# First layer's cross attention moved from the stacked, per-head loop to keys and values folded into its weights

## The chip, the cores and the metric

One core of one Trainium2 chip runs the whole program in a single launch. The metric is device time in microseconds, lower is better. The program is a two-layer decoder, and the change touches one of its six attention or expert stages, and a little of the stage behind it.

## The reference, cut to what matters

There are 4 batches of 512 tokens of width 128, and a context of 4 batches of 77 tokens of width 128. Each of the two layers does self attention, cross attention on the context and a mixture of experts, each added to its input and normalised. What the change touches is the first layer's cross attention and the norms behind it:

```python
def _L0_xattn_ref(q, k, v, Wq, bq, Wk, bk, Wv, bv, Wo, bo):   # HEADS = 16, DK = 8; k = v = the context
    qp = (q @ Wq + bq).reshape(b, s, HEADS, DK).transpose(0, 2, 1, 3)
    kp = k @ Wk + bk                       # (b, 77, 8): one key and one value head, shared by all 16
    vp = v @ Wv + bv
    scores = jnp.einsum('bhqd,bkd->bhqk', qp, kp)
    attn = jax.nn.softmax(scores, axis=-1)
    out = jnp.einsum('bhqk,bkd->bhqd', attn, vp)
    return out.transpose(0, 2, 1, 3).reshape(b, s, d) @ Wo + bo
...
x = _layernorm(x + _L0_xattn_ref(x, ctx_1024, ctx_1024, ...), axis=-1)
# _L0_ffn_ref begins with attention(layer_norm(x, ln1_w, ln1_b), ...): a second norm, with weights
```

The second layer's cross attention has 16 heads of width 64 with their own keys and values, on the same context.

## The kernel before, in words

The stages run one after the other. Each is one or two blocks; a block is one program for each of the five engines, and ends when all engines have ended theirs. Six tags name the stages in the tiles: a, b, c for the first layer's self attention, cross attention and the attention inside its feed-forward part; f for its experts; d, e, g for the second layer's self attention, cross attention and experts. XT holds the activations with width on the partitions, X those with tokens on the partitions.

**Stage b before** is `narrow_cross_attention`, three blocks.
- `narrow_projections` computes the queries for 4 batches (a float32 matmul of 512 columns each), ScalarE adds the bias (L310), VectorE splits each float32 result into three bfloat16 parts (`split_parts`, L185 to L190: cast, subtract, cast, subtract, cast), SyncE stores the parts to device memory (L261) and loads them back as stacks with 8 rows of head width times 9 combinations of parts (`load_stacks`, L353). Beside it `cross_operands` makes keys and values, and GpSimd sets rows 96 to 127 of the key stack KX to 1.0 (L1139); stage c needs these ones, b does not.
- `narrow_cross` runs a hardware loop over 16 steps of 4 heads, 64 heads of 512 tokens in all: scores (L1204), maximum and subtraction (L1266, L1268), exponential (L1292), transposes by TensorE (L1250), copy out of PSUM (L1303), value products (L1237), then the end of a group, with transposes (L385) and a division (L394, L397).
- `finish` projects with Wo, adds X and the bias, does two norms for each batch, and transposes back into XT. `norm_scales` puts the reciprocal root on GpSimd (L858, L860).

**Stage c** starts with `narrow_projections` as well, for queries, keys and values. It has nothing beside it on GpSimd before.

**Stage e** is the form that b takes over: `wide_operands` (L1670 and on) folds keys into the query weights (A, 128 x 77 for each head and batch) and values into the output weights (U); CP holds what the query bias adds, in three bfloat16 parts. `flat_cross` then has 32 halves: a tile of 128 tokens by 8 heads. Its order is written out by hand. For each half h TensorE does `turn(h)`, five transposes (L1887), `score(h + 3)`, two float32 matmuls of 308 columns (L1877) each with a small bfloat16 one (L1879), and `weigh(h)`, five matmuls (L1897). VectorE does `lessen(h + 2)` (L1967, L1971), `total(h + 1)` (L1978, L1982) and each second half an addition to X (L1988). ScalarE does the copy out of PSUM (L1938) and the exponential (L1932), GpSimd the division (`normalise`, L1854). Behind each batch of 8 halves the norm of the batch before is put in between: `layer(b, 0)`, statistics (L1992, L1995), at half 2 of the next batch, `layer(b, 1)`, application (L2001), at half 3, and GpSimd does `rstd` (L1848, L1850) behind `normalise` of half 3. For the last batch all of it stands at the end. With `pre` set there are two norms: then `layer(b, 1)` applies the first and takes the statistics of the second, `layer(b, 2)` applies the second, at half 4, and GpSimd does both `rstd` behind `normalise` of half 3, in order. No stage used this path before.

Of the kernel before, what the change touches and what calls it, by code (L numbers as in the profile page):

```python
# [356 lines left out]
def gather_values(c, pool, t, first, s_pv, s_vg, cross_values=None, per_group=1):  # L357


    nc = c.nc  # L360
# [2 lines left out]
    if cross_values is None:
        for kt in range(QT):
            src = c.VN[:, bass.ds((t // GROUPS) * QT + kt, 1), bass.ds((t % GROUPS) * GH * HD8, GH * HD8)]
            last = nc.gpsimd.tensor_copy(c.VG[:, kt, :, 0:HD8], src.rearrange("p a (h d) -> p (a h) d", d=HD8))
    else:
        last = nc.gpsimd.tensor_copy(c.VG[0:SROWS, 0, 0:1, 0:HD8], cross_values[:, bass.ds(t // GROUPS, 1), :])
# [736 lines left out]


def cross_operands(c, tag, own, wk, bk, wv, bv, KX, VB):

    nc = c.nc
    GR = SROWS // HD8  # L1110
    WK = c.sb(f"{tag}_WK", [P, HD8], F32, own)
    WKR = c.sb(f"{tag}_WKR", [P, SROWS], F32, own)
    BK = c.sb(f"{tag}_BK", [SROWS, 1], F32, own)
    WV = c.sb(f"{tag}_oWV", [P, HD8], F32, own)
    BV = c.sb(f"{tag}_oBV", [KC, HD8], F32, own)
    G = c.sb(f"{tag}_G", [SROWS, GR], F32, own)
    MK = c.sb(f"{tag}_MK", [SROWS, NPART], F32, own)
    FULL = c.sb(f"{tag}_KF", [SROWS, B * KC], F32, own)
    PARTS = c.sb(f"{tag}_KP", [SROWS, NPART, B * KC], BF16, own)
    s_w, s_g, s_ops, s_k, s_v, s_split = (c.sem(f"{tag}_o{n}") for n in ("w", "g", "ops", "k", "v", "split"))  # L1120

    def load(sp):
        sp.dma_start(WK[:, :], wk).then_inc(s_w, 16)
        sp.dma_start(WV[:, :], wv).then_inc(s_w, 16)
        sp.dma_start(BV[:, :], row(bv, KC)).then_inc(s_w, 16)
        for g in range(NPART * NPART):
            sp.dma_start(BK[g * HD8:(g + 1) * HD8, :], col(bk)).then_inc(s_w, 16)

    def pool_part(pool):
        nc.gpsimd.memset(VB[:, :, :], 0.0)  # L1130
        nc.gpsimd.memset(G[:, :], 1.0).then_inc(s_g, 1)
        pool.wait_ge(s_g, 1)
        nc.gpsimd.affine_select(out=G[:, :], in_=G[:, :], compare_op=ALU.is_ge, fill=0.0, base=0,
                                pattern=[[-HD8, GR]], channel_multiplier=1).then_inc(s_g, 1)
        pool.wait_ge(s_g, 2)
        nc.gpsimd.affine_select(out=G[:, :], in_=G[:, :], compare_op=ALU.is_ge, fill=0.0, base=HD8 - 1,
                                pattern=[[HD8, GR]], channel_multiplier=-1).then_inc(s_g, 1)
        pool.wait_ge(s_g, 3)
        nc.gpsimd.memset(c.KX[SROWS:P, :, :], 1.0)  # L1139

    def tensor_part(pe):
        pe.wait_ge(s_w, 16 * 12)
        pe.wait_ge(s_ops, 2)
        nc.tensor.matmul(c.ps_s[0:SROWS, 2, 0:B * KC], WKR[:, :], c.CTT[:, :], start=True, stop=True).then_inc(s_k, 1)
        for b in range(B):
            last = nc.tensor.matmul(c.ps_t[0:KC, 0, b * HD8:(b + 1) * HD8], c.CTT[:, b * KC:(b + 1) * KC], WV[:, :],
                                    start=True, stop=True)
        last.then_inc(s_v, 1)

    def vector_part(dve):  # L1150
        ops, split = Chain(s_ops), Chain(s_split)
        dve.wait_ge(s_w, 16 * 12)
        ops.inc(nc.vector.memset(WKR[:, NPART * NPART * HD8:], 0.0))
        ops.inc(nc.vector.tensor_copy(
            WKR[:, 0:NPART * NPART * HD8].rearrange("p (g d) -> p g d", d=HD8),
            WK[:, :].rearrange("p (a d) -> p a d", a=1).broadcast_to([P, NPART * NPART, HD8])))
        dve.wait_ge(s_g, 3)
        g = G[:, 0:NPART * NPART].rearrange("p (i j) -> p j i", j=NPART)
        ops.inc(nc.vector.reduce_sum(MK[:, :], g, AX.X))
        dve.wait_ge(s_k, 1)  # L1160
        rows = NPART * NPART * HD8
        ops.inc(nc.vector.tensor_copy(FULL[:, :], c.ps_s[0:SROWS, 2, 0:B * KC]))
        ops.wait(dve)
        ops.inc(nc.vector.tensor_scalar(FULL[0:rows, :], FULL[0:rows, :], BK[0:rows, :], None, ALU.add))
        ops.wait(dve)
# [1208 lines left out]
```

## Time and profile before

| | us |
|---|---|
| median of 3 runs | 2275.23 (2266.92 to 2277.47) |
| profiled execution, its own time | 2271.61 |
| span of its trace | 2269.9 |
| mean granted TensorE clock | 0.897 of 2.4 GHz |
| stage b: projections, loop, finish | 376.87 to 558.22: 44.39, 101.20, 35.76 |
| projections of stage c | 558.22 to 628.0 |
| stage e: operands, flat loop | 1872.08 to 2053.36: 43.84, 137.44 |

Over the span TensorE is busy for 1775.7 us (78%), its weight loads for 1000.7, VectorE for 1384.8 (61%), ScalarE for 1032.5 (45%), GpSimd for 155.7 (7%). As stages follow one another, these shares say little of one stage. The windows by stage and the instructions in order of time are the views to read.

### The profile page before, as it was taken

How to read it: one execution, taken by the hardware profiler on the slowest of the kernel's cores; microseconds unless marked ns; L12 is line 12 of the kernel's file. 1: busy time of each engine (PE TensorE's matmuls, PEld its weight loads, DVE VectorE, ACT ScalarE, POOL GpSimd, SP SyncE). 2: the span in 40 equal slices, each digit the busy share in tenths (PEclk: the TensorE clock that was granted, in tenths of full speed). 3: DMA queues.
4: the chain of work that ended last, by engine and by line, in shares of the span. 5: the costliest groups of instructions: out<-in, count | busy, mean ns of one | idle time of the engine just before them, and what ended most of it. 6: DMA issues, size and time to landing. Idle time of an engine off the chain costs nothing. (4 is left out here: it accounts for less than half of the span.)

```text
span 2269.9 us, 33575 instructions
## 1 busy us (share of the span) xinstructions
PE 1775.7 (78%) x9665; PEld 1000.7 (44%) x9718; DVE 1384.8 (61%) x4754; ACT 1032.5 (45%) x1970; POOL 155.7 (7%) x281
## 2 busy tenths in 40 slices
PE   4177775584149668699994999999999977997997
PEld 2144443353013223367772444444444434665664
DVE  7388885565358557433335777777777763774445
ACT  3288881362016446433331555656665543332221
POOL 2000003001000000100002000000000001330000
PEclk7599996696659889889996999999999987998999
DMA  1543200510540330010001000000000001000000
GB/s 57 80 44 38 29 0 11 79 25 7 89 51 5 39 41 2 3 38 19 19 10 37 1 1 1 1 1 1 1 0 1 1 1 39 1 1 21 17 19 26
DMA packets 57636, 48.74 MB, mean 21 GB/s; under 512 B 12691, under 2 KB 53047, under 8 KB 57527
## 3 DMA queue, kind: packets, MB, share of 16 engines
q1 hardware_dynamic: 57527, 47.45, 13.0%
q8 instruction: 49, 0.80, 0.1%
q14 instruction: 60, 0.49, 0.1%
HBM read 38.30 MB, written 8.91 MB: 21 GB/s over the span
## 5 line engine op out<-in xcount | busy, mean ns | idle before, releaser
L1432 PE MATMUL ps_s<-d_KZ,d_Q 128*128 128x512 f32 x512 | 265.4, 601 | 16.1 <-issue 6.8
L1580 ACT ACTIVATE d_PR<-d_PR,d_NM 128x512 f32<-128x512 f32 x256 | 184.7, 721 | 189.9 <-DVE d_NM L1511 189.5
L557 DVE TENSOR_REDUCE c_NM<-ps_t 128x1 f32<-128x512 f32 x256 | 169.9, 688 | 96.7 <-PE ps_t L437 95.0
L1507 DVE CUSTOM_DVE_ANT_0 d_PR<-ps_s,d_BH 128x512 f32<-128x512 f32 x256 | 176.2, 688 | 61.5 <-PE ps_t L1440 44.7
L437 PE MATMUL ps_t<-KX,QX 96*128 (+1 forms) x256 | 107.6, 425 | 105.1 <-DVE c_IB L575 47.6
L2288 DVE SCALAR_TENSOR_TENSOR X<-ps_t,GATE,X 128x128 f32<-128x128 f32 x272 | 76.7, 344 | 185.1 <-PE ps_t L2213 185.1
L619 ACT ACTIVATE c_PT<-ps_s 128x1024 f32<-128x1024 f32 x128 | 130.4, 1024 | 126.2 <-PE ps_s L460 124.3
L1440 PEld LDWEIGHTS ps_t<-ident,d_PR 128*128 128x128 f32 x1024 | 121.3, 141 | 150.8 <-issue 132.6
L1587 ACT ACTIVATE d_PT<-ps_t 128x512 f32<-128x512 f32 x256 | 149.9, 586 | 50.6 <-PE ps_t L1440 49.0
L762 ACT ACTIVATE a_PR<-a_PR,a_NM 128x128 f32<-128x128 f32 (+3 forms) x256 | 129.8, 555 | 78.0 <-DVE a_NM L743 78.0
L1440 PE MATMUL ps_t<-ident,d_PR 128*128 128x128 f32 x1024 | 156.4, 275 | 10.1 <-ACT d_PT L1587 8.1
L672 PE MATMUL ps_t<-ident,a_PR 128*128 128x128 f32 x640 | 115.4, 289 | 50.5 <-ACT a_PT L686 38.1
L2250 ACT ACTIVATE f_HT<-ps_s,f_BE 128x512 f32<-128x512 f32 x128 | 87.8, 687 | 128.5 <-PE ps_s L2203 127.7
L2203 PE MATMUL ps_s<-XT,g_W 128*128 128x512 f32 x288 | 131.9, 601 | 1.7 <-DVE g_HT L2267 1.7
L1519 DVE TENSOR_SCALAR d_PR<-d_PR,d_RDEN 128x512 f32<-128x512 f32 x256 | 124.7, 487 | 9.0
L2213 PEld LDWEIGHTS ps_t<-f_W,f_HT 128*128 128x128 f32 x1024 | 119.2, 192 | 14.8 <-issue 14.6
L1452 PE MATMUL ps_v<-d_PT,d_VB 128*64 128x512 f32 x512 | 116.9, 598 | 5.6 <-ACT d_PT L1587 4.9
L2213 PE MATMUL ps_t<-f_W,f_HT 128*128 128x128 f32 x1024 | 119.3, 275 | 0.0
L2203 PE MATMUL ps_s<-XT,f_W 128*128 128x512 f32 x256 | 117.4, 603 | 0.6 <-DMA f_W<-in_L_ffn_w 0.6
L672 PEld LDWEIGHTS ps_t<-ident,a_PR 128*128 128x128 f32 x640 | 70.3, 142 | 96.2 <-ACT a_PT L686 48.0
L2248 ACT ACTIVATE g_GT<-ps_s 128x512 f32<-128x512 f32 x72 | 43.0, 597 | 141.9 <-PE ps_s L2203 141.8
L437 PEld LDWEIGHTS ps_t<-KX,QX 96*128 (+1 forms) x256 | 25.0, 98 | 183.6 <-issue 103.0
(330 smaller groups left out, 3118.2 us busy)
## 6 DMA issues: line engine op xcount, KB each, us to landing
QX<-split_parts SPq DMA_DIRECT2D x108, 128.0 KB
KX<-split_parts SPq DMA_DIRECT2D x72, 128.0 KB
f_W<-in_L_ffn_w SPq DMA_DIRECT2D x16, 256.0 KB, 3.1
split_parts<-a_PARTS SPq DMA_DIRECT2D x8, 384.0 KB, 10.3
split_parts<-c_PARTS SPq DMA_DIRECT2D x8, 384.0 KB, 11.0
g_W<-in_L_ffn_w SPq DMA_DIRECT2D x24, 128.0 KB, 2.2
split_parts<-b_PARTS SPq DMA_DIRECT2D x4, 384.0 KB, 10.7
X<-in_x SPq DMA_DIRECT2D x4, 256.0 KB
```

The source lines that it names most:

```text
L437: nc.tensor.matmul(c.ps_t[:, i % 2, :], QX[0:SROWS, bass.ds(head, 1), qt * P:(qt + 1) * P], KX[0:SROWS, bass.ds(head, 1), :], start=True, ...
L557: nc.vector.tensor_reduce(NM[:, qt, j:j + 1], c.ps_t[:, i % 2, :], AX.X, ALU.max, negate=True).then_inc(maxed, 1)
L619: nc.scalar.activation(PT[:, half, j, :, :], c.ps_s[:, 2 * (j % 2):2 * (j % 2) + 2, :], ACT.Exp).then_inc(exped, 1)
L672: last = nc.tensor.transpose(c.ps_t[:, qt % 2, kt * P:(kt + 1) * P], PR[:, j % 2, qt, kt * P:(kt + 1) * P], c.ident[:, :])
L762: nc.scalar.activation(PR[:, j % 2, qt, 0:k], PR[:, j % 2, qt, 0:k], ACT.Exp, bias=NM[:, j % 2, qt:qt + 1]).then_inc(exped, 1)
L1432: nc.tensor.matmul(c.ps_s[:, qt % 2, :], Q[:, p % 2, qt * P:(qt + 1) * P], KZ[:, p % 2, i % 2, :], start=True, stop=True).then_inc(scores, 1)
L1440: mm = nc.tensor.transpose(c.ps_t[:, qt % 2, kt * P:(kt + 1) * P], PR[:, i % 2, qt, kt * P:(kt + 1) * P], c.ident[:, :])
L1507: nc.vector.tensor_tensor_reduce(out=PR[:, h % 2, qt, :], in0=c.ps_s[:, qt % 2, :], in1=BH[:, h, S - P - qt * P:2 * S - P - qt * P], scale ...
L1580: nc.scalar.activation(PR[:, h % 2, qt, :], PR[:, h % 2, qt, :], ACT.Exp, bias=NM[:, h % 2, qt:qt + 1], accum_out=DEN[:, h % 2, qt:qt + 1] ...
L1587: nc.scalar.activation(PT[:, i // 2 % 2, i % 2, :, qt * P:(qt + 1) * P], c.ps_t[:, qt % 2, :].rearrange("p (k q) -> p k q", q=P), ACT.Copy ...
L2203: nc.tensor.matmul(c.ps_s[:, ch, :], W[:, (ch % CH) * P:(ch % CH + 1) * P], c.XT[:, b * S:(b + 1) * S], start=True, stop=True).then_inc(s_ ...
L2213: mm = nc.tensor.matmul(c.ps_t[:, b % 2, q * P:(q + 1) * P], HT[:, b % 2, ch, q * P:(q + 1) * P], W2[i][:, ch, :], start=(ch == 0), stop=( ...
```

## The change

Stage b becomes two blocks: `narrow_operands`, which is new, and `flat_cross` with `pre` set, so with its two norms in the loop. The projections, the stacks, the loop by heads and the finish of b go. The setting of KX rows 96 to 127 moves to GpSimd in the projections of stage c, where it is the block's first GpSimd instruction.

```diff
@@ narrow_self_attention (stage c calls it without rel, so causal is None)
-            tables = distance_tables(c, rel, *causal, brief) if causal else None
+            tables = distance_tables(c, rel, *causal, brief) if causal else Beside(
+                lambda sp: None, lambda pool: nc.gpsimd.memset(KX[SROWS:P, :, :], 1.0), lambda pe: None, lambda dve: None)
             narrow_projections(c, tag, brief, scratch, QX, KX, s_qx, wq, wk, wv, bq, bk, bv, qscale, beside=tables)
@@ cross_operands, narrow_cross, narrow_cross_attention: removed, as is the cross part of gather_values
@@ new
+def narrow_operands(c, tag, wq, bq, wk, bk, wv, bv, wo, A, CP, U):
...
+            def _(sp):
+                sp.dma_start(WKV[:, 0, :], wk).then_inc(s_w, 16)
+                sp.dma_start(WKV[:, 1, :], wv).then_inc(s_w, 16)
+                sp.dma_start(BKV[:, 0, :], row(bk, 1)).then_inc(s_w, 16)
+                sp.dma_start(BKV[:, 1, :], row(bv, 1)).then_inc(s_w, 16)
+                sp.dma_start(WQ[:, :], wq).then_inc(s_w, 16)
+                sp.dma_start(BQ[:, :], col(bq)).then_inc(s_w, 16)
+                sp.dma_start(WO[:, :], wo).then_inc(s_w, 16)
+                sp.wait_ge(s_split, SPLIT_OPS + 1)
+                for i in range(NPART):
+                    sp.dma_start(CP[i:i + 1, :, :, :].rearrange("a h b k -> a h (b k)"), CH[:, i, :]).then_inc(s_cp, 16)
+                sp.wait_ge(s_cp, 16 * NPART)
...
+            def _(pool):
+                nc.gpsimd.memset(ONE[:, :], 1.0).then_inc(s_one, 1)
+                nc.gpsimd.memset(MH[:, :], 1.0).then_inc(s_mask, 1)
...
+                pool.wait_ge(s_kvout, 1)
+                for b in range(B):
+                    if b >= 2:
+                        pool.wait_ge(s_a, b - 1)
+                    nc.gpsimd.tensor_tensor(KBD[:, b % 2, :, :], over_heads(KV[:, 0, b * KC:(b + 1) * KC], H),
+                                            masks(slice(0, H)), ALU.mult).then_inc(s_kbd, 1)
...
+            def _(pe):
+                pe.wait_ge(s_w, 16 * 7)
+                nc.tensor.transpose(c.ps_f[:, 0:P], WQ[:, :], c.ident[:, :]).then_inc(s_wqt, 1)
+                pe.wait_ge(s_rep, 4)
+                pe.wait_ge(s_one, 1)
+                for w in range(2):
+                    nc.tensor.matmul(c.ps_s[:, w, 0:K2], WREP[:, w, :, :].rearrange("p h d -> p (h d)"), c.CTT[:, :],
+                                     start=True, stop=False)
+                    nc.tensor.matmul(c.ps_s[:, w, 0:K2], BREP[:, w, :, :].rearrange("p h d -> p (h d)"), ONE[:, :],
+                                     start=False, stop=True).then_inc(s_kv, 1)
+                pe.wait_ge(s_kvout, 1)
+                pe.wait_ge(s_bqm, 1)
+                nc.tensor.matmul(c.ps_v[0:H, 0:K2], BQM[:, :], KV[:, 0, :], start=True, stop=True).then_inc(s_c, 1)
...
+                for b in range(B):
+                    pe.wait_ge(s_kbd, b + 1)
+                    if b:
+                        pe.wait_ge(s_aout, b)
+                    for q in range(4):
+                        mm = nc.tensor.matmul(c.ps_s[:, q, 0:4 * KC], WQT[:, :],
+                                              KBD[:, b % 2, 4 * q:4 * q + 4, :].rearrange("p h k -> p (h k)"),
+                                              start=True, stop=True)
+                    mm.then_inc(s_a, 1)
+                    pe.wait_ge(s_vbd, 2 * (b + 1))
+                    if b:
+                        pe.wait_ge(s_uout, 2 * b)
+                    for i in range(2 * CHUNKS):
...
+                        mm = nc.tensor.matmul(dst, VBD[:, b % 2, i // CHUNKS, (i % CHUNKS) * P:(i % CHUNKS + 1) * P],
+                                              WO[:, :], start=True, stop=True)
+                    mm.then_inc(s_u, 1)
...
+            def _(act):
+                act.wait_ge(s_kv, 1)
+                nc.scalar.activation(KV[:, 0, :], c.ps_s[:, 0, 0:K2], ACT.Copy).then_inc(s_kvout, 1)
...
+                for b in range(B):
+                    act.wait_ge(s_a, b + 1)
+                    nc.scalar.activation(A[:, b, :, :].rearrange("p (q m) k -> p q (m k)", q=4), c.ps_s[:, :, 0:4 * KC],
+                                         ACT.Copy).then_inc(s_aout, 1)
...
+            def _(dve):
+                split = Chain(s_split)
+                dve.wait_ge(s_w, 16 * 7)
+                for w in range(2):
+                    nc.vector.tensor_copy(WREP[:, w, :, :], WKV[:, w:w + 1, :].broadcast_to([P, H, HD8])).then_inc(s_rep, 1)
+                    nc.vector.tensor_copy(BREP[:, w, :, :], BKV[:, w:w + 1, :].broadcast_to([1, H, HD8])).then_inc(s_rep, 1)
...
+                def values(b):
+                    if b >= 2:
+                        dve.wait_ge(s_u, b - 1)
+                    for half in range(2):
+                        nc.vector.tensor_tensor(
+                            VBD[:, b % 2, half, 0:HH * KC].rearrange("p (h k) -> p h k", k=KC),
+                            over_heads(KV[:, 1, b * KC:(b + 1) * KC], HH), masks(slice(half * HH, (half + 1) * HH)),
+                            ALU.mult).then_inc(s_vbd, 1)
+
+                def products(b):
+                    dve.wait_ge(s_u, b + 1)
+                    nc.vector.tensor_copy(U[:, b, 0:8, :].rearrange("p (a i) d -> p a (i d)", a=2), c.ps_t[:, :, :]).then_inc(s_uout, 1)
...
+                products(3)
+                split.wait(dve)
+                split_parts(nc, dve, split, CF[:, :], lambda i: CH[:, i, :])
@@ decoder
-            narrow_cross_attention(c, "b", a["L0_xattn_Wq"], a["L0_xattn_bq"], a["L0_xattn_Wk"], a["L0_xattn_bk"],
-                                   a["L0_xattn_Wv"], a["L0_xattn_bv"], scratch)
-            finish(c, "b", "ctx", wo=a["L0_xattn_Wo"], bias=a["L0_xattn_bo"], pre=(a["L0_ffn_ln1_w"], a["L0_ffn_ln1_b"]))
+            with ExitStack() as own:
+                A, CP, U = flat_operand_tiles(c, "b", own)
+                narrow_operands(c, "b", *(a[f"L0_xattn_{n}"] for n in ("Wq", "bq", "Wk", "bk", "Wv", "bv", "Wo")), A, CP, U)
+                flat_cross(c, "b", A, CP, U, a["L0_xattn_bo"], pre=(a["L0_ffn_ln1_w"], a["L0_ffn_ln1_b"]))
```

`flat_cross` itself is not changed.

## Rows read from the trace of the kernel before

**Rows 1.** Windows: us, then busy us (x instructions) of each engine, clock, DMA share, GB/s.
```profile
376.87:421.26 44.39, 8.72 (x18) 4.10 (x18) 24.39 (x35) 2.75 (x4) 14.30 (x5) 0.54 0.35 64
421.26:522.46 101.20, 83.97 (x704) 55.10 (x704) 65.33 (x160) 67.26 (x144) 6.49 (x17) 0.91 0.28 36
522.46:558.22 35.76, 12.85 (x64) 9.79 (x64) 23.43 (x104) 5.50 (x8) 10.13 (x16) 0.63 0.02 4
1872.08:1915.92 43.84, 30.16 (x160) 19.62 (x160) 13.79 (x32) 16.29 (x34) 0.40 (x2) 0.83 0.19 49
1915.92:2053.36 137.44, 126.18 (x688) 83.71 (x688) 93.58 (x192) 44.83 (x68) 49.20 (x46) 0.93 0.01 1
1917.30:1933.80 16.50, 15.93 (x43) 8.35 (x43) 9.11 (x14) 2.74 (x4) 8.00 (x7) 0.51 0.01 4
1938.00:1967.00 29.00, 29.00 (x171) 19.60 (x170) 21.13 (x37) 10.97 (x17) 9.72 (x8) 1.00 0.00 1
```

**Rows 2.** Instructions in order of time, stage b's projections and the start of c's.
```profile
377.81 13.75 POOL L1139 MEMSET KX<- 32x16384 bf16 x1
382.32 9.52 DVE L185 CAST b_PARTS<-b_FULL 128x512 bf16<-128x512 f32 x1 [2.76 <-ACT b_FULL L310]
...
558.22 1.28 SPq L251 DMA_DIRECT2D c_W<-in_L_ffn_w_qkv  x3
563.43 0.50 PEld L283 LDWEIGHTS ps_s<-XT,c_W 128*128 128x128 f32 x2 [6.69 <-DMA c_BV<-in_L_ffn_b_qkv]
566.33 0.43 DVE L185 CAST c_PARTS<-c_FULL 128x512 bf16<-128x512 f32 x1 [2.76 <-ACT c_FULL L310]
```

**Rows 3.** Instructions in order of time, stage e's operands.
```profile
1882.29 1.40 PE L1694 MATMUL ps_s<-CTT,e_Wk 128*128 128x308 f32 x2 [11.10 <-DMA e_Bv<-in_L_xattn_bv]
1883.48 1.23 PE L1698 MATMUL ps_s<-CTT,e_Wv 128*128 128x308 f32 x2
1887.69 0.52 ACT L1745 ACTIVATE e_KT<-ps_s,e_Bk 128x308 f32<-128x308 f32 x1 [1.18 <-PE ps_s L1694]
1898.93 0.31 DVE L185 CAST e_CH<-e_CF 16x308 bf16<-16x308 f32 x1
1900.96 1.84 SPq L1680 DMA_DIRECT2D e_CP<-e_CH  x3
```

**Rows 4.** DMA issues: count, KB each, median us from issue to landing.
```profile
e_CP<-e_CH SPq DMA_DIRECT2D x3, 9.6 KB, 1.9
```

**Rows 5.** Instructions in order of time, stage e's loop where the first norm is put in.
```profile
1969.21 0.58 PEld L1887 LDWEIGHTS ps_t<-ident,e_PR 128*128 128x128 f32 x5
1970.94 1.97 DVE L2001 TENSOR_SCALAR X<-X,e_MV,e_RS 128x128 f32<-128x128 f32 x4
1971.10 1.22 POOL L1854 TENSOR_TENSOR e_PR<-e_PR,e_RDEN 128x616 f32<-128x616 f32 x1 [1.10 <-DVE e_RDEN L1982]
1971.66 1.19 PEld L1897 LDWEIGHTS ps_f<-e_U,e_PT 128*128 128x128 f32 x10
1972.77 0.58 PEld L1887 LDWEIGHTS ps_t<-ident,e_PR 128*128 128x128 f32 x5
1976.74 0.53 PEld L1887 LDWEIGHTS ps_t<-ident,e_PR 128*128 128x128 f32 x5 [0.32 <-POOL e_PR L1854]
```

**Rows 6.** Instructions in order of time, stage b's finish: two norms in a row.
```profile
536.11 1.08 DVE L867 TENSOR_SCALAR X<-b_fR,b_fMV,b_fRS 128x128 f32<-128x128 f32 x4
538.91 1.04 POOL L860 TENSOR_TENSOR b_fRS<-b_fRS,neghalf 128x4 f32<-128x4 f32 x1
546.46 1.04 POOL L860 TENSOR_TENSOR b_fRS<-b_fRS,neghalf 128x4 f32<-128x4 f32 x1
546.67 0.69 DVE L1012 TENSOR_TENSOR b_fR<-b_fR,b_fBO 128x512 f32<-128x512 f32 x1
```

**Rows 7.** Instructions in order of time, the end of stage e.
```profile
2047.43 0.87 DVE L1992 BATCH_NORM_STATS2 e_ST<-X 128x6 f32<-128x128 f32 x4
2050.20 1.11 DVE L2001 TENSOR_SCALAR X<-X,e_MV,e_RS 128x128 f32<-128x128 f32 x4 [1.47 <-POOL e_RS L1850]
```

More of the change, by code:

```diff
@@ L354, in load_stacks, with gather_values @@
                                  scratch[b, w, :, part, :].rearrange("(h d) t -> d h t", d=HD8)).then_inc(sem, 16)
-def gather_values(c, pool, t, first, s_pv, s_vg, cross_values=None, per_group=1):
+def gather_values(c, pool, t, first, s_pv, s_vg, per_group=1):
     nc = c.nc
@@ L362, in gather_values @@
         pool.wait_ge(s_pv, per_group * t)
[L363 to L368, printed above, removed]
+    for kt in range(QT):
+        src = c.VN[:, bass.ds((t // GROUPS) * QT + kt, 1), bass.ds((t % GROUPS) * GH * HD8, GH * HD8)]
+        last = nc.gpsimd.tensor_copy(c.VG[:, kt, :, 0:HD8], src.rearrange("p a (h d) -> p (a h) d", d=HD8))
     last.then_inc(s_vg, 1)
@@ L1089, in narrow_self_attention @@
     with ExitStack() as own:
+        nc = c.nc
         QX, KX = c.QX, c.KX
@@ L1104, in narrow_self_attention @@
             narrow_full_attention(c, tag, own, QX, KX, scratch, s_qx)
[L1107 to L1165, printed above, removed]
-        split_parts(nc, dve, split, FULL[:, :], lambda i: PARTS[:, i, :])
-        kx = KX[:, :, :].rearrange("p b k -> p (b k)")
-        ops.inc(nc.vector.tensor_scalar(kx, PARTS[:, 0, :], MK[:, 0:1], None, ALU.mult))
-        for i in (1, 2):
-            ops.wait(dve)
-            ops.inc(nc.vector.scalar_tensor_tensor(kx, PARTS[:, i, :], MK[:, i:i + 1], kx, ALU.mult, ALU.add))
-        dve.wait_ge(s_v, 1)
-        nc.vector.tensor_tensor(VB[0:KC, :, :], c.ps_t[0:KC, 0, 0:B * HD8].rearrange("p (b d) -> p b d", b=B),
-                                BV[:, :].rearrange("p (a d) -> p a d", a=1).broadcast_to([KC, B, HD8]), ALU.add)
-    return Beside(load, pool_part, tensor_part, vector_part)
@@ L1312, in narrow_cross_attention @@
-def narrow_cross_attention(c, tag, wq, bq, wk, bk, wv, bv, scratch):
-    with ExitStack() as own:
-        QX = c.QX
-        KX = c.sb(f"{tag}_KX", [SROWS, B, KC], BF16, own)
-        VB = c.sb(f"{tag}_VB", [SROWS, B, HD8], F32, own)
-        s_qx = c.sem(f"{tag}_qx")
-        with ExitStack() as brief:
-            operands = cross_operands(c, tag, brief, wk, bk, wv, bv, KX, VB)
-            narrow_projections(c, tag, brief, scratch, QX, None, s_qx, wq, None, None, bq=bq, beside=operands)
-        narrow_cross(c, tag, own, QX, KX, VB, scratch, s_qx)
@@ L2315, in decoder @@
             finish(c, "a", "ctx", wo=a["L0_attn_Wo"], bias=a["L0_attn_bo"])
-            narrow_cross_attention(c, "b", a["L0_xattn_Wq"], a["L0_xattn_bq"], a["L0_xattn_Wk"], a["L0_xattn_bk"],
-                                   a["L0_xattn_Wv"], a["L0_xattn_bv"], scratch)
-            finish(c, "b", "ctx", wo=a["L0_xattn_Wo"], bias=a["L0_xattn_bo"], pre=(a["L0_ffn_ln1_w"], a["L0_ffn_ln1_b"]))
+            with ExitStack() as own:
+                A, CP, U = flat_operand_tiles(c, "b", own)
+                narrow_operands(c, "b", *(a[f"L0_xattn_{n}"] for n in ("Wq", "bq", "Wk", "bk", "Wv", "bv", "Wo")), A, CP, U)
+                flat_cross(c, "b", A, CP, U, a["L0_xattn_bo"], pre=(a["L0_ffn_ln1_w"], a["L0_ffn_ln1_b"]))
             q, k, v = (slice(i * P, (i + 1) * P) for i in range(3))
```

185 lines of the change are left out of this document (67 added, 118 removed).

## The prediction

> **What bounds the kernel now.** I read the windows first, cut at the first instruction of each stage. The stages don't overlap, so a stage's length counts in full. Stage b takes 44.39 + 101.20 + 35.76 = 181.35 us [rows 1]. None of its three blocks is bound by one engine alone all through: the projections have VectorE busy 24.39 of 44.39 us and wait for DMAs; the loop has TensorE busy 83.97 of 101.20 at a granted clock of 0.91; the finish is a chain, with TensorE at 12.85 and VectorE at 23.43 of 35.76. All of this the change removes.
>
> The same windows hold what takes its place, since stage e runs the same loop with the same 32 halves and the same sizes: 43.84 us of operands and 137.44 us of flat loop [rows 1]. There TensorE is busy 126.18 of 137.44 us, and 29.00 of 29.00 us in an undisturbed stretch at full clock. So the flat loop goes at TensorE's pace, a half every 1972.77 - 1969.21 = 3.56 us [rows 5].
>
> Then I read the instructions in order of time. In b's projections one cast of VectorE takes 9.52 us, where c's same cast takes 0.43 us. It ends at 391.84, just behind GpSimd's setting of KX, which runs from 377.81 to 391.56 [rows 2]. VectorE's cast stood still while GpSimd wrote.
>
> **The change part by part.**
>
> *Removed:* 181.35 us, with its stacks, its group ends and that stalled cast.
>
> *Operands of b.* Times from the block's start.
> - Loads: c's six DMAs let TensorE start 563.43 - 558.22 = 5.2 us behind the first issue [rows 2]. Here are seven; one more issue makes 5.4. Bounds 4 and 6.
> - Four small VectorE copies of up to 128 columns stand before the first product. The trace has no such copy; nearest is the 308-column cast at 0.31 [rows 3], so 4 x 0.25 = 1.0; between 0.5 and 1.3.
> - Keys: two accumulating products of 308 columns. At the low clock one follows another after 1883.48 - 1882.29 = 1.19 us [rows 3]: 2.4 us, and 0.6 with ScalarE's 0.52 copy [rows 3]. Keys are there at 9.4.
> - GpSimd spreads the first batch's keys over the heads: 1232 elements in each partition; `normalise` takes 1.22 us for 616 [rows 5], so 2.4. TensorE can begin at 11.8. The value products, at most another 2.4 us, and their copy lie beside this.
> - For each batch TensorE makes A, 4 products of 308 columns, 4 x 0.6 = 2.4 us at the high clock, half of 1.19 each; and U, ten of 128 columns: five take 1972.77 - 1971.66 = 1.11 us in `weigh` [rows 5], so 2.2. That is 4.6 at the high clock, 9.2 at the low one. e's operands begin at the low clock and run at 0.83 on the mean [rows 1]; I take one batch low and three high: 9.2 + 13.8 = 23.0, so 34.8. ScalarE's and VectorE's copies of a batch (1232 and 1024 elements, each about twice a 616-element operation) hide beside the other product. GpSimd's 2.4 for each batch hides as well.
> - VectorE spreads the values: eight operations of 616 elements, each 0.69 x 616 / 512 = 0.8 us [rows 6], beside GpSimd's four. Here the two might bar each other. Free, it costs 0. If each of the eight waits its turn behind GpSimd and TensorE for them, it costs 8 x 0.8 = 6.4. I take 1.5: 36.3.
> - Tail: copy of the last U, 1.2; five operations on the bias part, 1900.96 - 1898.93 = 2.0; three DMA issues 1.84 [rows 3], and the last one's landing, 1.9 less its own issue's 0.6 [rows 4]; 0.5 for the change of block. 6.8 us, and nothing covers it: in e the same DMAs are issued at 1900.96 with 15 us of work behind them, here `split_parts` stands last on VectorE.
>
> Sum 43.1 us. The lowest: high clock from the start (keys 1.2 less, first batch 4.6 less), no barring: 36. The highest: all four batches at the low clock (13.8 more) and 4.9 more of barring: 61, reached hardly ever. e's operands took 43.84, so I stay at 43.
>
> The Trainium skill has a rule on that barring (SBUF — State Buffer, section "Who interferes with whom"): a VectorE instruction with two SBUF inputs contends with a GpSimd instruction that reads SBUF, and the loser waits for all of the other. The nearest row speaks against it, but weakly: at 546.67 VectorE adds two SBUF tiles in its usual 0.69 us while GpSimd runs a 4-element operation from 546.46 to 547.50 [rows 6]. By the rule the operands would take up to 4.9 us more, 48; by the row, 1.5 us less.
>
> *Flat loop of b.* 137.44 us as in e [rows 1], e's 16.5 us at the low clock at its start included. Three things are added.
> - End: behind the last batch stands one more norm. In e statistics to application take 2050.20 - 2047.43 = 2.8 us and the application 1.1 [rows 7]; with 0.2 for the biased copy into XT that is 4.1.
> - Norms within the loop, three times. At half 3, GpSimd does normalise(3), the first `rstd`, then the second `rstd`, and only then normalise(4). The second waits for VectorE: application of the first norm, statistics, then GpSimd's power. In the finish this chain takes from 536.11 to 538.91 + 1.04 = 539.95, 3.84 us [rows 6]. In e the application starts at 1970.94 [rows 5], so here the second `rstd` would end at 1974.78 and normalise(4), 1.22, at 1976.0, where it now ends at 1972.3. Queued behind it are turn(4) and by that all of TensorE: 1976.1 for 1972.77. e's own 0.4 us delay at the next half (3.97 for 3.56) [rows 5] falls inside it, so the loss is 3.3 - 0.4 = 2.9 us, three times: 8.7. VectorE has the spare time for the rest (busy 21.13 of 29.00 [rows 1]).
> - Clock: before each of these turns TensorE now idles some 3 us. Nothing in e's loop waits that long. If the clock falls, the time at the low clock costs nearly half of itself. From 0 to 3 x 8 = 24 (e's low stretch: 16.5 us, half lost [rows 1]); I take 3, as a short drop in one or two of them.
>
> 137.4 + 4.1 + 8.7 + 3 = 153.2.
>
> *Start of c.* KX is now set by GpSimd's first instruction there: 558.22 + 13.75 = 572.0 in old times. VectorE's first cast would start at 566.33 and end at 566.76 [rows 2]; barred as in b, it ends 0.28 behind GpSimd, at 572.25: 5.5 us. All stores and stack loads hang on the later casts, so nothing covers it. That gives back part of the 9.1 us stall that went with b's projections. Bounds 0 and 5.5; I take 5.5, as VectorE and the operation are the same.
>
> **Sum.** 43.1 + 153.2 - 181.4 + 5.5 = +20.4 us. On the profiled execution's own 2271.6 us that is 2292. The median before is 3.6 us above that execution; I don't add it. I predict 2292 us, 0.9% slower. In short, the flat loop at 3.56 us for each half costs more than the narrow loop and its finish together (153 against 137), and the operands save next to nothing on the projections (43 against 44).
>
> **Rivals.**
> - *Not slower: stage b at TensorE's own pace, at 2.4 GHz.* The place is all of stage b; it decides once 20 us go. Operands at their low end, 36 (7 less); no low stretch at the loop's start (8 less); no norm stall and no drop (11.7 less). -26.7 in all: 2265. For it: the undisturbed 29 us of e. Against: e itself started low twice [rows 1], and the chain of the two norms is a fixed order on GpSimd. 5%.
> - *The norms don't hold up TensorE.* 8.7 and 3 go: 2280. It needs normalise(4) to come early enough, and in the rows it is already 0.4 us from being late. 13%.
> - *The clock falls at each stall and stays low as long as in e's start.* +21: 2313. For it: b's loop has idle stretches and a clock of 0.91. 12%.
> - *Operands at the low clock and barred.* Their new waits between GpSimd and TensorE could keep the clock down: 43 becomes 55, so 2304. 12%.
> - *The setting of KX is free in c.* If the stall in b had another cause, 5.5 go: 2286. 7%.
>
> **How the numbers follow.** The forecast has 51%, its own range 2284 to 2300 from the operands' bounds near e and the clock term. The range takes in the neighbours: 2277 to 2310. A measurement of this kernel can tell about 0.5% from no change, 11.4 us. Slower by more is the forecast, most of it, the low clock and barred cases and much of the KX one: 0.73. Within it are the norms without a stall, the first rival and the low tail of the forecast: 0.23. Faster by more: 0.04, for something that no row shows.
>
> **What would show it.** Windows of stage b: 43 and 153 us. In the flat loop, at halves 12, 20 and 28, a turn that starts some 6.9 us behind the one before, with GpSimd named as releaser, and GpSimd's wait for the second statistics just before. At the start of c one cast of about 5.9 us that ends with the setting of KX. In the operands, TensorE idle for 2 us or so before the first A, and nothing on any engine but the bias part and its DMAs in the last 5 us. Wrong would be: operands under 36 or over 50, a loop under 145, a cast of 0.43 us in c, or a low clock through several halves behind each norm.

## The result, and the profile after

| | before | after |
|---|---|---|
| median, on the same chip | 2273.11 us (6 runs) | 2289.76 us (6 runs, 2280.74 to 2295.81) |
| ratio of the times | | 1.0072, 95% interval [1.0048, 1.0097] |
| profiled execution, its own time | 2271.61 | 2280.74 |
| span of its trace | 2269.9 | 2279.0 |
| stage b in all | 181.35 | 37.48 + 157.92 = 195.4 |
| projections of c | 69.9 | 75.4 |
| loop of c | 307.5 | 302.3 |

The change makes the kernel 0.7% slower: 16.7 us by the medians. The profiled executions differ by only 9.1 us, because in this one c's loop, which the change does not touch, was 5.2 us shorter. The result lies inside the predicted range, 2 us below the forecast of 2292. A second series, x11 below, gave a ratio of 1.0075.

The first view is the windows of the changed kernel: operands of b, flat loop of b, projections and loop of c, then three stretches of operands and loop, chosen by the granted clock (columns as in [rows 1]).

```profile
375.86:413.34 37.48, 26.18 (x123) 18.49 (x123) 14.31 (x23) 7.35 (x11) 10.28 (x9) 0.77 0.02 5
413.34:571.26 157.92, 133.86 (x688) 88.77 (x688) 103.42 (x240) 45.18 (x68) 54.05 (x54) 0.87 0.00 1
571.26:646.67 75.41, 15.61 (x48) 8.99 (x48) 28.51 (x45) 5.50 (x8) 13.75 (x1) 0.61 0.44 77
646.67:949.02 302.35, 229.79 (x1664) 80.04 (x1664) 183.03 (x385) 148.63 (x160) 12.59 (x64) 0.85 0.21 24
...
378.00:390.00 12.00, 9.66 (x17) 4.19 (x18) 3.42 (x9) 1.02 (x3) 4.47 (x2) 0.50 0.05 12
390.00:406.50 16.50, 16.50 (x108) 14.30 (x106) 7.91 (x9) 5.94 (x7) 4.90 (x2) 0.97 0.00 1
...
472.00:478.80 6.80, 6.54 (x23) 4.36 (x24) 4.72 (x10) 1.31 (x2) 1.38 (x2) 0.56 0.00 0
509.50:512.90 3.40, 3.40 (x13) 2.06 (x12) 2.42 (x6) 1.13 (x2) 0.14 (x1) 0.62 0.00 0
543.70:553.90 10.20, 9.41 (x38) 7.24 (x37) 5.26 (x11) 2.62 (x4) 3.05 (x3) 0.54 0.00 0
```

The first two answer to b's three windows in [rows 1]. In the operands the clock is at its low level up to 390 and at its high one from there, so all but the first 2.8 us of the products for the four batches (they start at 387.24) run at 2.4 GHz. The last three windows lie in the flat loop, close behind three stalls of TensorE: the clock goes from the high level (2.4 GHz) to the low one (1.2 GHz, 0.50 of full speed) for 6.8, 3.4 and 10.2 us. Looked at in windows of 1 us, it falls at 472.8, 510.3 and 544.5, each time 0.5 to 1.8 us after TensorE has gone back to work, so a window above holds a little of the high level too.

Next, instructions in order of time, where the first norms are put into b's loop. This is the same place as e's in [rows 5].

```profile
465.22 1.04 POOL L1791 TENSOR_TENSOR b_RS<-b_RS,neghalf 128x4 f32<-128x4 f32 x1
...
467.19 1.07 DVE L1942 TENSOR_SCALAR X<-X,b_MV,b_RS 128x128 f32<-128x128 f32 x4
...
468.29 0.87 DVE L1933 BATCH_NORM_STATS2 b_ST<-X 128x6 f32<-128x128 f32 x4
469.20 0.38 DVE L1936 BATCH_NORM_AGGREGATE b_MV<-b_ST 128x2 f32<-128x6 f32 x4
...
469.67 0.23 POOL L1789 TENSOR_SCALAR b_RS<-b_MV 128x4 f32<-128x4 f32 x1 [3.40 <-DVE b_MV L1936]
469.98 1.04 POOL L1791 TENSOR_TENSOR b_RS<-b_RS,neghalf 128x4 f32<-128x4 f32 x1
...
470.99 2.39 POOL L1795 TENSOR_TENSOR b_PR<-b_PR,b_RDEN 128x616 f32<-128x616 f32 x2
...
472.26 0.53 PEld L1828 LDWEIGHTS ps_t<-ident,b_PR 128*128 128x128 f32 x5 [3.15 <-POOL b_PR L1795]
```

Read it from the bottom. TensorE's next turn waits for GpSimd's `normalise`. That stands behind the second reciprocal root (a TENSOR_SCALAR and the power behind it), which waits 3.40 us for VectorE's second statistics, and those wait for VectorE's application of the first norm. Turn follows turn here after 6.79 us instead of 3.56; at halves 20 and 28 after 6.79 and 6.80.

The end of the operands:

```profile
406.56 1.23 DVE L1711 COPY b_U<-ps_t 128x1024 f32<-128x1024 f32 x1 [3.08 <-PE ps_f L1665]
407.70 0.30 DVE L185 CAST b_CH<-b_CF 16x308 bf16<-16x308 f32 x1
...
409.71 1.88 SPq L1613 DMA_DIRECT2D b_CP<-b_CH  x3
413.34 0.35 SPq L1772 DMA_DIRECT2D b_BO<-in_L_xattn_bo  x1
...
413.78 0.85 PE L1818 MATMUL ps_s<-b_A,XT 128*128 128x308 f32 x1 [7.26 <-POOL b_PR L1780]
```

TensorE is idle for 7.26 us between its last value product and the loop's first score. The split of the bias part and its DMAs are all that happens. And the start of c, which answers to [rows 2]:

```profile
571.27 13.75 POOL L1098 MEMSET KX<- 32x16384 bf16 x1 [3.48 <-POOLq L1769]
...
580.23 5.07 DVE L185 CAST c_PARTS<-c_FULL 128x512 bf16<-128x512 f32 x1 [2.76 <-ACT c_FULL L310]
```

The cast ends at 585.30, 0.28 us behind GpSimd's write (585.02), as b's did before.

### The profile page after: what moved, and what is told of

It reads as the page before. It is cut to its first block and busy times, and to the rows that moved or that the text cites. A ratio compares the mean times of both kernels' runs of the same rounds, so it can differ in the third digit from the quotient of the medians.

```text
span 2279.0 us, 32904 instructions
## 1 busy us (share of the span) xinstructions
PE 1837.7 (81%) x9743; PEld 1040.7 (46%) x9743; DVE 1394.4 (61%) x4718; ACT 1008.3 (44%) x1893; POOL 202.7 (9%) x307
## 5 line engine op out<-in xcount | busy, mean ns | idle before, releaser
L2154 PEld LDWEIGHTS ps_t<-f_W,f_HT 128*128 128x128 f32 x1024 | 119.2, 192 | 14.8 <-issue 14.6
```

The lines of the kernel that those rows point to most:

```text
L2154: mm = nc.tensor.matmul(c.ps_t[:, b % 2, q * P:(q + 1) * P], HT[:, b % 2, ch, q * P:(q + 1) * P], W2[i][:, ch, :], start=(ch == 0), stop=( ...
```

## The experiments

All ratios are to the kernel before, on the same chip.

| kernel | what differs | median us (runs) | ratio, 95% interval |
|---|---|---|---|
| x1_reorder | after, second reciprocal root and second application one half later | 2274.93 (10) | 1.0018 [0.9994, 1.0041] |
| x2_warm | after, TensorE kept busy in the norm stall | 2282.27 (6) | 1.0060 [1.0035, 1.0085] |
| x3_early | after, bias split earlier | 2285.52 (8) | 1.0070 [1.0050, 1.0091] |
| x4_pieces | after, KX set in 32 pieces | 2287.28 (5) | 1.0073 [1.0043, 1.0103] |
| x5_all | after, all three, improved | 2262.99 (8) | 0.9958 [0.9944, 0.9973] |
| x6_before_pieces | before, KX in 32 pieces | 2260.72 (9) | 0.9957 [0.9939, 0.9976] |
| x7_before_moved | before, KX set at c's start | 2267.83 (10) | 0.9975 [0.9957, 0.9993] |
| x8_tail | x5, TensorE kept busy behind its last product | 2262.28 (7) | 0.9955 [0.9939, 0.9970] |
| x11_after | after again | 2286.43 (10) | 1.0075 [1.0049, 1.0101] |
| x12_all_again | x5 again | 2264.00 (12) | 0.9964 [0.9946, 0.9983] |
| x13_pieces_again | x6 again | 2263.45 (12) | 0.9964 [0.9945, 0.9982] |

**x1_reorder: does the order on GpSimd make the stall?**

```diff
-                    if h % (2 * QT) == 3 and h > 3:
-                        for k in range(norms):
-                            rstd((h // (2 * QT) - 1) * norms + k)
+                    if h % (2 * QT) in (3, 4)[:norms] and h > 4:
+                        rstd((h // (2 * QT) - 1) * norms + h % (2 * QT) - 3)
...
-                    if h > 3 and h % (2 * QT) in (2, 3, 4, 5)[:1 + norms] and h >= 2 * QT:
-                        layer(h // (2 * QT) - 1, h % (2 * QT) - 2)
+                    due = (2, 3, 5)[:1 + norms]
+                    if h % (2 * QT) in due and h >= 2 * QT:
+                        layer(h // (2 * QT) - 1, due.index(h % (2 * QT)))
```

> The second reciprocal root moves behind normalise of half 4, and VectorE's application of the second norm from half 4 to half 5. Theory (order on GpSimd): the turns of halves 12, 20 and 28, which start 6.8 us behind the ones before in the changed kernel, come after 3.6 to 4.0 us; the low-clock halves behind them go too, since TensorE no longer idles. The flat loop of stage b goes from 157.9 to 141 to 146 us, the whole 12 to 16 us below the changed kernel. Rival (VectorE's work is the wait: the second norm's statistics and application don't fit in, wherever GpSimd stands): the stall only moves to the next half, the loop stays above 153.

The loop took 149.8 us for 157.9, less of a gain than expected. Turns 12, 20 and 28 follow after 3.56 us. But the next ones take 5.26, 5.26 and 5.27. TensorE's wait stands in the last instruction below, and its cause two engines further up; the window behind it is from the third of these places to the loop's end:

```profile
466.51 1.97 DVE L1941 TENSOR_SCALAR X<-X,b_MV,b_RS 128x128 f32<-128x128 f32 x4
468.52 0.87 DVE L1932 BATCH_NORM_STATS2 b_ST<-X 128x6 f32<-128x128 f32 x4
...
469.72 0.77 DVE L1907 TENSOR_REDUCE b_M<-ps_s 128x8 f32<-128x616 f32 x1
...
473.61 0.53 PEld L1827 LDWEIGHTS ps_t<-ident,b_PR 128*128 128x128 f32 x5 [1.61 <-POOL b_PR L1795]
...
536.30:562.40 26.10, 12.97 (x53) 10.68 (x53) 9.82 (x36) 4.27 (x6) 5.45 (x8) 0.52 0.00 0
```

The norms hold VectorE in one go from 466.51 to 469.72, and its work for the next half comes that much later. So GpSimd's order was the larger cause, and behind it stood a second one, on VectorE, that my working had not seen. The clock stayed high behind the first two waits and was low from the third one to the end.

**x2_warm: what does the clock cost?** Twelve products without use are issued ahead of the turn that stalls.

```diff
+                    if norms == 2 and h % (2 * QT) == 4 and h > 4:
+                        for i in range(12):
+                            nc.tensor.matmul(c.ps_t[:, 1, 3 * P:4 * P], c.ident[:, :], c.ident[:, :], start=True, stop=True)
```

> The order stays, but TensorE runs 12 products of the identity with itself, into an unused part of PSUM, in each of the three stalls of about 3 us. Theory (part of the loss is the clock, which falls behind each idle stretch): the stall stays at 6.8 to 7.2 us from turn to turn, but the two halves behind it, which took 6.0 and 4.3, 4.9 and 3.7, 5.3 and 4.4 us, take 3.6 to 3.9 each; the loop goes from 157.9 to 151 to 154. Rival (the halves behind the stall are late because VectorE's and GpSimd's work has piled up): they stay as long, and the loop at 157 to 159.

The stall itself stays: 6.79 us from turn to turn at all three places. What changes is the half behind it: 3.51 us, where after has 5.96, 4.89 and 5.34. In order of time and by window:

```profile
469.50 2.84 PE L1826 MATMUL ps_t<-ident 128*128 128x128 f32 x24
...
472.62 0.53 PEld L1831 LDWEIGHTS ps_t<-ident,b_PR 128*128 128x128 f32 x5 [0.47 <-POOL b_PR L1795]
...
413.70:563.50 149.80, 133.83 (x760) 90.94 (x760) 103.25 (x240) 45.18 (x68) 54.03 (x54) 0.91 0.01 1
...
428.00:551.00 123.00, 117.42 (x720) 82.91 (x719) 91.64 (x205) 41.63 (x63) 44.08 (x43) 1.00 0.00 1
```

From 428 to 551 the clock is high without a break. The loop is 157.9 - 149.8 = 8.1 us shorter. With the stall unchanged, that is what the low clock cost; if anything a little more, since in x2 the last products of the loop ran at the low clock, which fell at 551.5, and in after they did not. The times of the whole kernel are too coarse to show it: the ratios are 1.0060 here and 1.0072 and 1.0075 for after, 3 us apart, and each is uncertain by 0.25%, 6 us.

**x3_early: is the tail worth its 6.8 us?** `split_parts` stands between `values(2)` and `products(1)` on VectorE, so that the three DMAs go out while TensorE still works.

> The bias part is split behind the values of the third batch, not last, so its three DMAs run beside the products. Theory (nothing covers the tail): the operands go from 37.5 to 32.0 to 33.0 us, 5 us less. Rival (the block's end waits for something else, such as the last copies): 36 us or more. A further rival: the five operations now hold up the copy of U and by that TensorE, 35 us.

```profile
376.70:410.90 34.20, 26.54 (x123) 18.47 (x123) 16.39 (x23) 7.35 (x11) 10.27 (x9) 0.78 0.03 6
...
396.70 2.65 POOL L1632 TENSOR_TENSOR b_KBD<-b_KV,b_Mh 128x1232 f32<-128x1232 f32 x1 [2.06 <-PE ps_s L1656]
...
397.13 2.38 DVE L185 CAST b_CH<-b_CF 16x308 bf16<-16x308 f32 x1
...
402.61 2.02 PE L1665 MATMUL ps_t<-b_Wo,b_VBD 128*128 128x128 f32 x16 [1.69 <-DVE b_U L1711]
```

The operands take 34.2 us for 37.5. The cast that took 0.30 us in the tail now takes 2.38, until GpSimd has spread its keys; the copy of U behind it comes late, and TensorE waits 1.69 us. So the tail goes, and part of it comes back. The loop was 161.5 us here, at a mean clock of 0.84 where after's had 0.87: behind the three norm stalls, which are the same, the clock was low for 6.8, 6.8 and 13.6 us, 27.2 in all for after's 20.4. So the clock took what was left of the gain. The ratio is that of after.

**x4_pieces: the setting of KX.**

```diff
-                lambda sp: None, lambda pool: nc.gpsimd.memset(KX[SROWS:P, :, :], 1.0), lambda pe: None, lambda dve: None)
+                lambda sp: None, lambda pool: [nc.gpsimd.memset(KX[SROWS:P, i, :], 1.0) for i in range(2 * H)],
+                lambda pe: None, lambda dve: None)
```

> The ones in KX are written at c's start in 32 instructions of 512 elements (0.43 us each) in place of one of 13.75 us. Theory (VectorE's cast waits for a GpSimd instruction that is under way): c's first cast goes from 5.07 us to at most 0.9, other casts grow by up to 0.4, and c's projections go from 75.4 to 70 to 72.5 us. Rival (GpSimd's writes bar VectorE for as long as they last in all, in whatever pieces): the first cast still ends when GpSimd ends, projections at 75. Second rival (the cast was late for another reason): no change either.

From the view of the tile c_PARTS (durations in ns: least, median, most), x4 and then after:

```profile
L185 DVE CAST c_PARTS<-c_FULL x8: 416/427/742, 583.2 to 606.4; 128x512 bf16<-128x512 f32 x8
```
```profile
L185 DVE CAST c_PARTS<-c_FULL x8: 417/422/5069, 580.2 to 607.1; 128x512 bf16<-128x512 f32 x8
```

The longest cast is 0.74 us, and c's projections take 71.2 us for 75.4. Most of the 5.5 us is back. Of the 1.3 us that are left, 0.9 have nothing to do with GpSimd: TensorE starts 6.05 us behind the block's start, when the loads have landed, where it was 5.2 before. The rest is some casts that meet a piece (0.74, 0.57 and 0.71 us for 0.43). The time alone, over 5 runs, shows nothing of it.

**x5_all: all of it, with what x1 and x3 taught.** VectorE's second statistics get a half of their own, and the split stands where GpSimd has nothing left to do. KX is set as in x4. Cut to the edits that differ from x1's, x3's and x4's:

```diff
-                products(2)
-                products(3)
                 split.wait(dve)
                 split_parts(nc, dve, split, CF[:, :], lambda i: CH[:, i, :])
+                products(2)
+                products(3)
...
+                    if h % (2 * QT) in (3, 5)[:norms] and h > 5:
+                        rstd((h // (2 * QT) - 1) * norms + (h % (2 * QT) - 3) // 2)
...
+                    due = (2, 3, 4, 6) if norms == 2 else (2, 3)
```

> Three changes to the changed kernel at once. Norms: VectorE applies the first at half 3, takes the second's statistics at half 4, applies it at half 6; GpSimd does the second reciprocal root behind normalise of half 5. Operands: the bias part is split between the last values and the copy of the third U. Stage c: KX in 32 instructions. Theory (each loss has its own cause and they add): operands 33 us (37.5 in the changed kernel), flat loop 144 to 147 us (157.9), c's projections 71 us (75.4); the whole 2267 to 2273 us, level with the kernel before. With only the reordering of the roots, the turn of half 13 came 5.26 us behind that of 12, since VectorE did application and statistics together; now 3.6 to 4.2. Rival (what is taken away comes back as a wait at the next place, the transposes back at half 7): loop over 149 us.

```profile
378.30:410.40 32.10, 26.13 (x123) 18.49 (x123) 14.31 (x23) 7.35 (x11) 10.30 (x10) 0.77 0.03 6
410.40:553.70 143.30, 123.92 (x688) 83.57 (x688) 104.92 (x240) 45.85 (x68) 54.09 (x54) 0.94 0.01 1
553.70:624.90 71.20, 14.85 (x48) 8.88 (x48) 24.56 (x45) 5.50 (x8) 16.95 (x33) 0.60 0.47 81
```

Against after, the operands lose 5.4 us, the loop 14.6 and c's projections 4.2, 24.2 together; by the two ratios the kernels are 0.0114 x 2273 = 26 us apart. Turns 12 to 14 follow after 3.56, 3.97 and 3.81 us. The three losses add, as the theory says, but the whole came out 4 us below its expected range (2262.99, with 2267 to 2273 expected), so this version beats both kernels where it was expected level with the one before. The stages explain half of that: operands, loop and c's projections take 246.6 us together, 4.6 less than the 181.35 + 69.9 = 251.2 of before, and the medians are 10 us apart.

**x6_before_pieces and x7_before_moved: was it the fold that x5 profits from?** Both are the kernel before, with only its setting of KX changed: in 32 pieces where it stood, or whole at c's start.

```diff
-        nc.gpsimd.memset(c.KX[SROWS:P, :, :], 1.0)
+        for i in range(2 * H):
+            nc.gpsimd.memset(c.KX[SROWS:P, i, :], 1.0)
```

> The kernel before, with the ones in KX written in b's projections in 32 instructions of 512 elements. Theory (VectorE's cast waited for one long GpSimd instruction): the cast of 9.52 us takes at most 0.9, b's projections go from 44.4 to 35 to 37 us, the whole 7 to 9 us below the kernel before, about 2263. Rival (the projections end with the DMAs, whose last landing took 18.8 us, and these don't start earlier by as much): 40 us or more.

> One part of the change alone: the kernel before, with the setting of KX moved whole from b's projections to the start of c's. Theory: b's projections 44.4 to 35 to 36 us, c's 69.9 to 75, since c's first cast ends with GpSimd's 13.75 us; net 3 to 4 us faster than before. Rival (b's stall had another cause, such as a load): b's projections stay at 44, c's get longer, net 5 us slower.

The first fence is x6, the second x7, each with b in all and c's projections:

```profile
377.20:549.90 172.70, 108.69 (x786) 71.67 (x786) 105.09 (x299) 75.57 (x156) 35.56 (x69) 0.76 0.26 38
549.90:618.60 68.70, 13.51 (x48) 7.90 (x48) 23.87 (x45) 5.50 (x8) 0.00 (x0) 0.60 0.47 84
```
```profile
377.50:547.70 170.20, 106.12 (x786) 70.42 (x786) 103.86 (x299) 75.13 (x156) 17.22 (x37) 0.77 0.26 39
547.70:622.60 74.90, 15.57 (x48) 8.84 (x48) 29.39 (x46) 5.50 (x8) 13.80 (x2) 0.59 0.44 77
...
555.83 5.92 DVE L185 CAST c_PARTS<-c_FULL 128x512 bf16<-128x512 f32 x1 [2.76 <-ACT c_FULL L310]
```

In x7 the stall leaves b's projections (44.39 to 35.3 us, 9.1 gained) and stands at c's start (5.0 lost, with one cast of 5.92 us): 4.1 us net, as expected. That is the effect of the change's memset alone, with the narrow form kept. The median has 5.7 (0.0025 x 2273), and b as a whole is 11.1 us shorter, because its loop took 98.1 us for 101.2 of before. It took 100.9 in x6 and 99.3 in x13, and goes with the mean granted clock (0.95, 0.91, 0.91, 0.94), not with an edit. In x6 b's projections take 34.8 us, b gains 8.6 us in all, and c loses nothing. No cast of x6's b waits long any more (the one of 9.52 us was among these four):

```profile
L185 DVE CAST b_PARTS<-b_FULL x4: 454/712/712, 382.7 to 392.0; 128x512 bf16<-128x512 f32 x4
```

A loop over 32 pieces is worth as much as all that x5 gets.

**x8_tail: does a busy TensorE keep the clock up into the loop?** Nine products without use stand behind the last value product of x5.

> As the kernel with all three changes, and TensorE runs nine products of the identity with itself behind the last U, while the operands' block ends. Theory (the low clock of the loop's first 17 us comes from TensorE's idle time at the operands' end): the clock stays high into the loop, the first turns come 3.6 us apart in place of 5.3 to 6.4, and the loop gets 4 to 7 us shorter. Rival (the clock falls at the loop's start for another reason, such as its own first halves waiting for VectorE and GpSimd): low from about 413 as before, no gain.

It made no difference: the ratio is 0.9955 beside 0.9958. The theory had taken the 17 us at the low clock from after's loop, and x5's loop doesn't have them: it starts at the high clock, though TensorE idles for 1.98 us just before it. So there was nothing for the products to keep up. In both, TensorE waits some 3.5 us in the loop's first half for the first `normalise`, and then the clock is low for 6.8 us. The first fence is x5, the second x8:

```profile
420.00 0.95 PE L1828 MATMUL ps_t<-ident,b_PR 128*128 128x128 f32 x5 [3.45 <-POOL b_PR L1796]
...
419.60:426.40 6.80, 6.40 (x22) 4.21 (x23) 2.39 (x4) 1.31 (x2) 1.52 (x2) 0.56 0.00 0
```
```profile
419.26 1.33 PE L1830 MATMUL ps_t<-ident,b_PR 128*128 128x128 f32 x5 [3.46 <-POOL b_PR L1798]
...
418.10:424.90 6.80, 5.64 (x17) 3.46 (x18) 1.97 (x4) 1.31 (x2) 2.28 (x2) 0.58 0.00 0
```

**x11_after, x12_all_again, x13_pieces_again: c's loop, and the two forms side by side.** No edits: after, x5 and x6 again, all on one chip.

> The changed kernel as it stands, a second time, for the spread of stage c's loop (302.3 us in the profiled run of it, 307.5 in that of before; 302 to 314 over all profiles taken so far). Theory: that loop's length changes from run to run and has nothing to do with the change, so in this profile it lies anywhere from 302 to 314 us, while operands (37.5), stage b's loop (157.9) and c's projections (75.4) come out within 1 us of the first profile, except where a low clock falls elsewhere in the loop (up to 4 us). Ratio 1.005 to 1.010. Rival: the change itself shortens c's loop by some 5 us; then it lies at 302 to 304 again.

> x5_all again, on one chip with x13_pieces_again, to compare the two forms of layer 0's cross attention with each one's stalls taken away. Theory: the folded form is worth nothing here even then: by the profiles b and c's projections last 246.6 us together in x5_all and 241.4 in x6_before_pieces, so this kernel comes out 0 to 5 us behind x13, ratio 0.995 to 0.998. Rival: the folded form is the faster one once its stalls are gone: 3 us or more ahead of x13.

> x6_before_pieces again beside x12_all_again. Theory: ratio 0.993 to 0.997, 0 to 5 us ahead of x12. Rival: 3 us or more behind it.

Operands, flat loop and c's projections came out at 37.50, 158.00 and 74.7 us, so they repeat; c's loop took 304.9. x12 and x13 tie at 0.9964. Their stages differ as forecast: b and c's projections together take 246.9 us in x12 and 241.5 in x13. That this does not show in the medians is no wonder with intervals of 0.2% on each side (4 us): x12's stages are 4.3 us under the 251.2 of before, and its ratio stands for 8.

What makes c's loop differ, the waits of TensorE in it show (line: waited for, us in total, times, longest). Before, after, and x8, which has the longest loop:

```profile
PE ps_t L437 <- DMA KX<-split_parts: 42.2, 2, 22.4
PE ps_s L460 <- DMA QX<-c_MX: 19.5, 1, 19.5
```
```profile
PE ps_t L434 <- DMA KX<-split_parts: 38.4, 2, 19.2
PE ps_s L457 <- DMA QX<-c_MX: 17.1, 1, 17.1
```
```profile
PE ps_t L434 <- DMA KX<-split_parts: 50.0, 2, 25.9
PE ps_s L457 <- DMA QX<-c_MX: 17.9, 1, 17.9
```

TensorE waits for loads of the stacks: 61.7, 55.5 and 67.9 us. Each loop less these waits is 307.5 - 61.7 = 245.8, 302.3 - 55.5 = 246.8 and 313.8 - 67.9 = 245.9. Over all thirteen profiles the loops run from 302.2 to 313.8 us, and what is left from 245.2 to 247.4. So the spread is in the waits for these loads, in both forms alike. Why one execution's loads are quicker than another's is open.

## Why the prediction was right, point by point

| term | forecast | measured | |
|---|---|---|---|
| removed | -181.4 | -181.4 | |
| operands of b | 43.1 | 37.5 | 5.6 too much |
| flat loop as in e | 137.4 | 137.1 | 157.9 less the next three |
| norm at the end | 4.1 | 4.2 | from VectorE's last addition to the next block 10.4 in b, 6.25 in e |
| norm stall | 8.7 | 8.5 | three halves in x2 against e's |
| low clock behind the stalls | 3 | 8.1 | x2 |
| start of c | 5.5 | 5.5 | windows, 75.4 - 69.9 |
| sum | +20.4 | +19.5 | medians +16.7 |

- **The frame was right.** The flat loop costs more than the narrow loop and its finish, and the operands save little. Two errors of 5 us with opposite signs, 5.6 too much in the operands and 5.1 too little in the clock, left the sum good. That is luck: by the size of its terms it deserved less.
- **Operands, 5.6 too much.** TensorE starts 4.3 us behind the block's start, not 5.4, and the small copies take 0.21 to 0.23 us each, not 0.25. Little of that is left at the first A, 11.4 us behind the start for 11.8: GpSimd has its keys spread at about 386.4, but TensorE is still at the value and bias products until 387.2, which the working had put beside the path. So the idle 2 us of TensorE before the first A, one of the signs, did not come. The larger part is TensorE's own: from the first A to the last U, 387.24 to 406.5, it needs 19.3 us where I had 23.0 and 1.5 for barring. The clock rose at 390, inside the first batch, where I had taken the whole batch low. The tail was 6.8 us, exactly as worked out from e's rows [rows 3, 4]. The rival "at the low clock and barred" is wrong.
- **Barring between VectorE and GpSimd.** It happens, but beside the path. Of the eight spreads of values one takes 1524 ns instead of 790: the first, issued at 387.74 while GpSimd's second spread runs to 388.61. Of GpSimd's four one takes 2651 instead of 2256: it is issued at 395.75 while VectorE's runs to 396.28. TensorE did not wait for either. The Trainium skill (SBUF — State Buffer, section "Who interferes with whom") says that a VectorE instruction with two SBUF inputs contends with a GpSimd instruction that reads SBUF; these rows agree, and the row that I set against it [rows 6], a 4-element operation, was too weak. By the rule I would have added 4.9 us, and its real price here was 0. x3 shows that the price depends on what waits behind.
- **Norm stall.** Its mechanism and its place are as forecast: the turn came 3.23 us later (6.79 for 3.56), where I had 3.3, with the releaser named. In x2, where the clock stays up, that half and the two behind it take 6.79 + 3.51 + 3.56 = 13.86 us. In e the same three take 3.97 + 3.51 + 3.56 = 11.04, with the late turn of [rows 5]. That is 2.8 us each, as the 2.9 of the working. The rival "the norms don't hold up TensorE" is wrong.
- **Clock, the term that was mis-sized.** I took 3 us, "as a short drop in one or two". It fell at all three, for 6.8, 3.4 and 10.2 us, and cost 8.1. The bounds, 0 to 24, held it. The stalls were dearer by their echo than I had allowed: 8.5 us of waiting brought another 8.1. The rival that gave it the length of e's start each time (+21) went too far. At the third stall the clock was low through two halves (5.34 and 4.36 us), which comes near the sign "a low clock through several halves behind each norm" that was to show the forecast wrong. And the length of a stall alone does not set the price: e's loop of before began its 17 us at the low clock behind 1.4 us of waiting, and x5's, where TensorE's waits in the last batch had been 0.86 us at most, was low for 3.4 us as well, from 536.7 on.
- **Start of c.** It cost 5.5 us by the windows, with a cast of 5.07 us (5.9 forecast; the loads let the work start later than before, TensorE at 577.34, 6.1 us behind the block's start, not 5.2, and the cast ends with GpSimd's write either way). x4 and x7 show that it is GpSimd's write: in pieces it leaves no cast longer than 0.74 us, and moved by itself into c it makes the same stall there.
- **The profiled execution** is 9.1 us longer than the one of before, not 19.5. Of the 10.4 us between, 5.2 are c's loop, by its loads; the rest is spread over the other stages, none with more than 2.3.
- **What I missed** is that the best change was in the rows that I had read. I wrote that the cast "stood still while GpSimd wrote", 9.1 us lost, and treated it as a debit of the old form. It is a stall that a loop takes away, and x6 gains 0.4% by that alone.

## What to carry to other kernels

When a part is rewritten, ask of each stall in the old form whether it belongs to the form; here 9 of the old form's 181 us were a wait for a GpSimd write that could be cut into pieces, and with that done in both forms the folded one is level by the medians and 5 us longer by its stages (x12, x13). In a loop ordered by hand, a second small chain between two engines is better spread over the turns, so that no in-order queue waits within one: the two waiting instructions here took 1.3 us, and what was queued behind them came 3.2 us late each time, and in this loop as much again went with the clock. TensorE's waits for three stack loads in c's loop, 56 to 68 us, are several times the size of anything that this change moves.
